# A causal attention layer's step order: exponentials and maxima taken before the step's long matmul unit, key copies issued by SP, normalized rows stored in two parts

## The reference

```python
x = x + layernorm(attention(layernorm(x)))      # 16 query heads of 32, one key/value head, causal
x = x + layernorm(moe(layernorm(x)))            # 8 experts, top 2, and a shared expert
# attention: q = xn @ q_w.T + q_b ; k, v likewise (32 wide)
#   scores = q k^T / sqrt(32), later keys masked ; softmax ; times v ; @ o_w.T + o_b
```

## Time and profile before

| | us |
|---|---|
| median of 3 runs | 2262.08 |
| profiled execution, its own time | 2262.99 |
| its span, first to last instruction | 2261.2 |
| attention, from the page's slices and the timeline | 0 to about 892 |
| routing, experts, shared expert | about 892 to 2261 |
| TensorE busy in the whole span | 2015.1 (89%) |
| VectorE, ScalarE, GpSimd busy | 1043.0, 713.6, 468.7 |
| mean granted TensorE clock | 0.946 of full |

### The profile page before, as it was taken

One profiled execution on the slowest core, in us unless ns is written; L12 is line 12 of the kernel. 1 busy time (PEld: TensorE's weight loads), 2 busy tenths in 40 slices (PEclk: granted clock), 3 DMA queues, 4 the chain that ended last, 5 costly groups with the idle time before them and its releaser, 6 DMA issues. The chain is left out here.

```text
span 2261.2 us, 30875 instructions
## 1 busy us (share of the span) xinstructions
PE 2015.1 (89%) x10858; PEld 1534.2 (68%) x10858; DVE 1043.0 (46%) x2158; ACT 713.6 (32%) x1350; POOL 468.7 (21%) x1044
## 2 busy tenths in 40 slices
PE   4988989888888982399999999999999999999995
PEld 3655555565555541377788788878888888888884
DVE  3555655565555533744454555534424333233243
ACT  2434444444444341143433344422111111111111
POOL 1223232332423232111101111000121120220212
PEclk9799999999999986599998999999999999999998
DMA  5133351615243221434443555443120230221202
GB/s 172 51 98 114 99 164 67 193 53 159 84 129 112 84 94 74 152 102 171 162 174 138 190 171 186 145 168 97 46 103 19 94 112 19 94 73 48 103 19 93
DMA packets 107018, 250.36 MB, mean 111 GB/s; under 512 B 10752, under 2 KB 25344, under 8 KB 99616
## 3 DMA queue, kind: packets, MB, share of 16 engines
q1 hardware_dynamic: 92064, 207.73, 26.9%
q0 software_dynamic: 11520, 37.76, 5.3%
q10 hardware_dynamic: 3328, 3.41, 0.7%
HBM read 165.76 MB, written 79.69 MB: 109 GB/s over the span
## 5 line engine op out<-in xcount | busy, mean ns | idle before, releaser
L1223 PE MATMUL ex_bank<-ex_xT,ex_gu 128*128 128x512 f32 (+14 forms) x1656 | 345.5, 367 | 5.0 <-DVE ex_xT L1257 5.0
L1223 PEld LDWEIGHTS ex_bank<-ex_xT,ex_gu 128*128 128x128 f32 (+1 forms) x1656 | 277.1, 183 | 69.3 <-DVE ex_xT L1257 5.4
L632 DVE TENSOR_REDUCE at_nmax<-at_bank 128x1 f32<-128x384 f32 (+3 forms) x512 | 229.7, 479 | 123.3 <-PE at_bank L407 122.9
L1273 DVE TENSOR_TENSOR sh_silu<-sh_silu,sh_bank 128x512 f32<-128x512 f32 x88 | 60.6, 688 | 457.6 <-ACT sh_silu L1266 451.0
L1223 PE MATMUL sh_bank<-sh_xT,sh_gate 128*128 128x512 f32 x1056 | 255.4, 391 | 6.8 <-DVE sh_dn L1679 5.2
L1235 PE MATMUL sh_bank<-sh_dn,sh_act 128*128 128x512 f32 x1056 | 254.3, 390 | 0.0
L1223 PE MATMUL sh_bank<-sh_xT,sh_up 128*128 128x512 f32 x1056 | 253.6, 389 | 0.0
L827 ACT ACTIVATE at_PT<-at_bank 128x512 f32<-128x512 f32 (+1 forms) x384 | 194.7, 515 | 175.8 <-PE at_bank L420 164.4
L1266 ACT ACTIVATE sh_silu<-sh_bank 128x512 f32<-128x512 f32 x88 | 52.7, 599 | 592.4 <-PE sh_bank L1223 547.0
L1223 PEld LDWEIGHTS sh_bank<-sh_xT,sh_gate 128*128 128x128 f32 x1056 | 199.0, 189 | 49.4 <-issue 8.1
L1235 PEld LDWEIGHTS sh_bank<-sh_dn,sh_act 128*128 128x128 f32 x1056 | 197.6, 188 | 43.7 <-DVE sh_act L1282 2.9
(11 more groups left out here) (227 smaller groups left out, 2581.6 us busy)
## 6 DMA issues: line engine op xcount, KB each, us to landing
ex_gu_in<-gu_in SPq DMA_DIRECT2D x23, 1408.0 KB, 9.2
at_Qs<-q_dram SPq DMA_DIRECT2D x96, 256.0 KB, 4.7
ys<-sh_yk SPq DMA_DIRECT2D x17, 1024.0 KB
q_dram<-at_q_h SPq DMA_DIRECT2D x64, 256.0 KB, 3.6
xnT<-at_xT SPq DMA_DIRECT2D x16, 1024.0 KB, 5.7
sh_xT<-xnT SPq DMA_DIRECT2D x16, 1024.0 KB
ex_dn_in<-dn_in SPq DMA_DIRECT2D x23, 512.0 KB, 9.6
at_x_in<-x_in SPq DMA_DIRECT2D x8, 1024.0 KB, 5.3
```

The source lines that it names most:

```text
L632: last = nc.vector.tensor_reduce(nmax[:, s % 2, i:i + 1], S_ps[u][:, col:col + (i + 1) * P], AX_X, ALU.max, negate=True)
L1223: last = self.nc.tensor.matmul(self.gate_up_ps[c % 2][which][0:m, 0:w], cols(i, k), self.xT[j][:, k, 0:w], start=(step == 0), stop=(step = ...
L1273: nc.vector.tensor_tensor(silu[c % 2][0:m, 0:w], silu[c % 2][0:m, 0:w], gate_up_ps[c % 2][1][0:m, 0:w], ALU.mult).then_inc(s["product"], 1)
```

## The change

1. In the 12 steps that are not in `PAIRED` (steps 1, 2, 9 and 10, whose units come in two halves) VectorE takes the maxima of unit 2, and ScalarE the exponentials of unit 2, ahead of `first_low` and `first_high`.
2. `move_k` goes from ScalarE's program to SP's. For sequence 0 its six transfers come before the first `spill_q`. KsT of sequence b comes between `spill_q(b, 3)` and `move_q(b, 3)`; KsS of sequence b+1 between `move_q(b+1, 1)` and `spill_q(b+1, 2)`, behind a wait for the last query scores of sequence b.
3. In SP's list x_res is loaded after the stores of xnT and xn2; `move_q(b+1, 0)` comes before the store of x1; the store of xn2 of sequence b-2 stands in turn b behind that of xnT (before: of sequence b-1 in turn b, near the end).
4. ScalarE normalizes tiles 0 and 1 of x1 of sequence b-1 at the end of step 15 of turn b, and tiles 2 and 3 at the end of step 0 of turn b+1.

```diff
--- before.py
+++ after.py
@@ -269,6 +269,8 @@
 
         Q_STEP = {12: 0, 13: 1, 15: 2, 0: 3}
 
+        PAIRED = (1, 2, 9, 10)
+
         def head(b, s, lag):
             return (b, s - lag) if s >= lag else (b - 1, s - lag + H)
 
@@ -308,6 +310,11 @@
                 for half in range(2):
                     sp.dma_start(q_dram[half, c], q_h[c % 2][half][:].bitcast(F32)).then_inc(q_spilled[c], 16)
 
+            def move_k(n, Ks, moved):
+                for at, half in ((0, 0), (1, 0), (2, 1)):
+                    sp.dma_start(Ks[HD * at:HD * at + HD, :].bitcast(F32),
+                                  vk_h[half][HD:2 * HD, :].bitcast(F32)).then_inc(moved, 16)
+
             def move_q(n, c):
                 if has(n - 1):
                     sp.wait_ge(shifted, 3 * (H * (n - 1) + HG * (c + 1)))
@@ -318,6 +325,9 @@
 
             sp.wait_ge(xT1_ps, C)
             sp.dma_start(x_in[:], seq(x, 1)).then_inc(x_in_s, 16)
+            sp.wait_ge(qkv_lo, 1)
+            move_k(0, KsS, kS_moved)
+            move_k(0, KsT, kT_moved)
             spill_q(0, 0)
             spill_q(0, 1)
             move_q(0, 0)
@@ -327,35 +337,37 @@
             sp.wait_ge(w_split, 6)
 
             def turn(b):
-                if has(b - 1):
-                    if has(b - 2):
-                        sp.wait_ge(x1_ready, QT * (b - 1))
-                    sp.dma_start(x_res[:], seq(x, b - 1)).then_inc(x_res_s, 16)
                 if has(b):
                     spill_q(b, 3)
+                    if has(b - 1):
+                        sp.wait_ge(shifted, 3 * H * b)
+                        move_k(b, KsT, kT_moved)
                     move_q(b, 3)
                 if has(b - 2):
                     sp.wait_ge(xT2_lo, C * (b - 1))
                     for half in range(2):
                         sp.dma_start(xnT_out[bass.ds(b - 2, 1), half].rearrange("o p c t -> p (o c) t"),
                                      xT[half][:].bitcast(F32)).then_inc(xnT_stored, 16)
+                    sp.dma_start(seq(xn_out, b - 2), xn2[:]).then_inc(xn2_moved, 16)
+                if has(b - 1):
+                    if has(b - 2):
+                        sp.wait_ge(x1_ready, QT * (b - 1))
+                    sp.dma_start(x_res[:], seq(x, b - 1)).then_inc(x_res_s, 16)
                 if has(b + 2):
                     sp.wait_ge(xT1_ps, C * (b + 2))
                     sp.dma_start(x_in[:], seq(x, b + 2)).then_inc(x_in_s, 16)
                 if has(b + 1):
                     spill_q(b + 1, 0)
+                    move_q(b + 1, 0)
                 if has(b - 1):
                     sp.wait_ge(x1_ready, QT * b)
                     sp.dma_start(seq(x1_out, b - 1), y[:]).then_inc(x1_stored, 16)
                 if has(b + 1):
-                    move_q(b + 1, 0)
                     spill_q(b + 1, 1)
                     move_q(b + 1, 1)
+                    sp.wait_ge(scores, 3 * H * (b + 1))
+                    move_k(b + 1, KsS, kS_moved)
                     spill_q(b + 1, 2)
-                if has(b - 1):
-                    sp.wait_ge(xn_ready, QT * b)
-                    sp.dma_start(seq(xn_out, b - 1), xn2[:]).then_inc(xn2_moved, 16)
-                if has(b + 1):
                     move_q(b + 1, 2)
 
             turns(sp, turn)
@@ -751,10 +763,15 @@
                     maximum(b, s, 1)
                     norm_steps(b, s, 1)
                     spread_inverses(b, s)
-                    first_low(b, s)
-                    maximum(b, s, 2)
-                    norm_steps(b, s, 2)
-                    second_low(b, s)
+                    if s in PAIRED:
+                        first_low(b, s)
+                        maximum(b, s, 2)
+                        norm_steps(b, s, 2)
+                        second_low(b, s)
+                    else:
+                        maximum(b, s, 2)
+                        norm_steps(b, s, 2)
+                        first_low(b, s)
                     take_sums(b, s)
                     scale_mixed(b, s)
                     take_v(b, s)
@@ -790,12 +807,6 @@
                 staged, halves, _ = WEIGHTS[part]
                 act.wait_ge(w_in[part], 16)
                 nc.scalar.activation(halves[0][:], staged, ACT.Copy).then_inc(w_hi, 1)
-
-            def move_k(n, Ks, moved):
-                act.wait_ge(qkv_lo, 5 * n + 1)
-                for at, half in ((0, 0), (1, 0), (2, 1)):
-                    act.dma_start(Ks[HD * at:HD * at + HD, :].bitcast(F32),
-                                  vk_h[half][HD:2 * HD, :].bitcast(F32)).then_inc(moved, 16)
 
             high_weights(0)
             high_weights(1)
@@ -809,8 +820,6 @@
             scale_vk(0, bank[0])
             high_q(0, 0, bank[1])
             high_q(0, 1, bank[2])
-            move_k(0, KsS, kS_moved)
-            move_k(0, KsT, kT_moved)
             high_q(0, 2, bank[3])
 
             def exponentials(b, s, tb):
@@ -880,19 +889,17 @@
             def turn(b):
                 for s in range(H):
                     exponentials(b, s, 0)
-                    if s == 2 and has(b) and has(b - 1):
-                        act.wait_ge(shifted, 3 * H * b)
-                        move_k(b, KsT, kT_moved)
                     take_row(b, s)
                     high_mixed(b, s)
                     exponentials(b, s, 1)
                     move_row(b, s)
-                    first_high(b, s)
-                    exponentials(b, s, 2)
-                    second_high(b, s)
-                    if s == H - 1 and has(b + 1):
-                        act.wait_ge(scores, 3 * H * (b + 1))
-                        move_k(b + 1, KsS, kS_moved)
+                    if s in PAIRED:
+                        first_high(b, s)
+                        exponentials(b, s, 2)
+                        second_high(b, s)
+                    else:
+                        exponentials(b, s, 2)
+                        first_high(b, s)
                     if s in (7, 8) and has(b + 1):
                         for i in range(2 * s - 14, 2 * s - 12):
                             normalize(x_in, x_in, 0, b + 1, i, x_normed)
@@ -901,8 +908,11 @@
                             normalize(y, y, 1, b - 1, i, y_normed)
                     if s == H - 1 and has(b - 1):
                         act.wait_ge(xn2_moved, 16 * b)
-                        for i in range(QT):
+                        for i in range(2):
                             normalize(xn2, y, 2, b - 1, i, xn_ready)
+                    if s == 0 and has(b - 2):
+                        for i in range(2, QT):
+                            normalize(xn2, y, 2, b - 2, i, xn_ready)
 
             turns(act, turn)
 
```

## The result

| | before | after |
|---|---|---|
| median, us | 2263.73 (2256.04 to 2266.34, 4 runs) | 2193.14 (2189.26 to 2199.07, 4 runs) |
| profiled execution, its own time | 2262.99 | 2199.07 |
| its span | 2261.2 | 2197.3 |
| turns 1 to 7 | 690.3 | 633.2 |
| TensorE busy; mean granted clock | 2015.1; 0.946 | 1988.5; 0.948 |

The ratio is 0.9696 (95% interval 0.9661 to 0.9731): 3.0% faster, 70.6 us by the medians and 63.9 us by the two profiled executions. The forecast was 2188, 5 us lower. That is closer than its terms deserve: several were wrong by 10 to 25 us, in both directions.

A forecast was written before the change was run, and what follows sets the result against it. TensorE was taken as the pacer of attention, so only its idle or slow time could be gained; the terms summed to -74.6 us, taking 2263.0 to 2188 us, with a range of 2167 to 2214.

The forecast's parts named there:

- What bounds the kernel: Attention, turns 1 to 7: TensorE is the pacer, busy 599 of 690 us; later stages counted unchanged.
- Maxima ahead: VectorE in unpaired steps: TensorE's waits for maxima go, 35.6 us of 38.1; bounds 0 and 38.1.
- exponentials ahead: ScalarE in unpaired steps: key scores' waits for exponentials go, 17.2 us of 20.5; bounds 0 and 20.5.
- The high half moved behind costs nothing: ScalarE, unpaired steps: free, since its unit ends 2 to 3 us later than the exponential of 0.36 us.
- KsS by SP: Start of each turn: earlier key issue leaves about 1.0 us wait per turn, 9.6 of 16.6 us go.
- Rival 1: Keys stay as late as now, behind the queries in SP's queue; total 2205 us; chance 0.18.
- KsT and step 2: Steps 2 and 3: waits for KsT, the row and part of xT go, 7 us; bounds 0 and 10.7.
- The clock: project_q in steps 0 and 12: two thirds of 17.3 us of clock dips go, 11.5; bounds 5 and 17.3.
- First turn: Turn 0: SP issues the keys; 1.5 us off the 7.3 us wait for the first queries.
- Normalizing in two parts: Steps 0 and 1: two moved ACTIVATEs cost 0.85 us in turns 2 to 7, +5.1; bounds 0 and 9.2.
- Rows stored later: Last turn: xn's store behind both xnT parts delays the next stage by 2.7 us; bounds 2 and 4.3.
- Rivals 3 and 4: Rival 3 (0.10): VectorE takes the maximum's place in steps 5 to 8, 2202 us; rival 4 (0.05): SP queue bounds, slower.

The follow-up runs named there:

- the orders alone: Kernel before with only the VectorE and ScalarE orders changed (maxima and exponentials of unit 2 ahead of the long unit): 2206.11 us, ratio 0.9767.
- Keys first: Kernel after, with KsS ahead of move_q(b+1, 1) in SP's list instead of behind it: 2167.50 us, ratio 0.9598.
- two tiles ahead: Keys first, plus tiles 2 and 3 normalized ahead of high_q in step 0 and xn2 stored ahead of its transposes: 2161.94 us, ratio 0.9559.

## Why the prediction came out as it did

- *What bounds the kernel*: right. The stage behind attention hardly moved, and all of the gain lies in what TensorE spent idle or slow.
- *Maxima ahead, -35.6; exponentials ahead, -17.2*: the mechanism was right (steps 5 to 8 last 4.40 us, against 4.6 foretold, and L390's waits fell from 55 to 7), the sizes were not. The sum was made from recorded waits, and each stall costs about 0.2 us more than its record: steps 5 to 8 alone gave 20.3 us for 28 waits that sum to 14.4. Against that stood a cost that the prediction did not have: 9.8 us of waits stay at L402, where it left 1.1. 3.3 of them are the copies of keys and values under GpSimd's additions. Split between the two, the terms were far off: about 62 and 4 us, not 36 and 17, since each was priced as if the other wait had no part in it. "The high half moved behind costs nothing" was wrong twice: what comes after the earlier exponential falls on VectorE's copies, and the two tiles that are normalized behind the high half end too late for step 1.
- *KsS by SP, -9.6*: against the kernel before the wait grew by 6.2. Two things are in that: the orders alone, with shorter steps, made it 25.0, and SP's issue took off 6.1 (28.9 to 22.8, or 2.2 from the 25.0). The forecast left 1.0 us in each turn, and 3.3 stayed. The step that failed is "SP's queue still holds the queries of move_q(b+1, 1), 0.75 MB, issued at 413.1": that time was taken over from the trace of before, but the list was edited ahead of it. The second spill left 10.6 us ahead of turn 4 instead of 12.1 and stood behind 1.75 MB, its landing took 6.8 instead of 4.6 us, and the queries that wait for it left 3.7 us later in the turn, right ahead of the keys. The three issues took 1.8 us, not 1.3. Rival 1 had the place behind the queries, not the later issue, and was given 0.18; its total of 2205 was too high because the other terms were too small.
- *KsT and step 2, -7*: right. Its wait and that for the row are gone, step 2 lost 7.9 us, step 3 gained 0.3 with the wait for mixed_f.
- *The clock, -11.5*: step 12's share came (3.0 us in every turn, 5.4 saved, 1.1 of it in turn 0), step 0's did not (11.9 over became 10.3 over), since the wait ahead of it grew. Together 7.0. Keys first shows that it was there to be had.
- *First turn, -1.5*: the first query scores begin at 41.5 instead of 44.5 us and their wait is 6.1 instead of 7.3. With the shorter steps of turn 0, turn 1 begins 11.8 us earlier; the terms for this stretch (3.8 and 1.7 of the two orders' and 1.5) make 7.0.
- *Normalizing in two parts, +5.1*: right in sign, a little small: step 1 is 7.5 us longer in all, with the wait for xn in its row (4.2 us in 6); undoing the part took 6.2 of them back.
- *Rows stored later, +2.7*: right. GpSimd opens the next stage 2.77 us behind the last logits (823.73 to 826.50), before 0.54: 2.2 us.
- *Rivals 3 and 4*: VectorE took no place in steps 5 to 8 (no wait there), and the keys came about 3 us too late (5.2 at most), far from the 11.7 from which the change would cost time.

Against the profiled execution the sum was 10.7 us too low. The keys (15.8), the clock (4.5) and the normalizing (2.4) were put too well by 23 us; with the other terms at their measured sizes the two orders are left with about 57 us in turns 1 to 7 for 47 forecast there, 10 too few; what lies outside those turns gave 7.1 us (1.1 of it clock) for 4.3. The profiled execution is the slowest of its four, and the median forgave another 6. That the centre was near is in large part luck: terms that were 10 and more too large met terms that were as much too small.

## What to carry to other kernels

Where a queue's list is edited, work out the issue time of everything in it anew, and count the bytes that stand ahead of a small urgent transfer, those that hold up its predecessors' landings too: a late one at the turn's start takes back what is gained ahead of it (the exponentials' order gave nothing measurable with the keys late, and 4 us of turns without). Count a removed stall of TensorE a little above its record (0.2 us each here), and the clock behind a long one separately. Where two waits stand in one step, price them together: the second can take up what the first gives back. When an engine's work moves earlier, ask what it releases on a third engine, and on whose ports that falls.

## What was not expected of the hardware

- A stall of TensorE recorded as 0.47 us costs 0.70 us of the step; 28 of them, recorded as 14.4 us, cost 20.3.
- A cast of 64x512 fp32 within SBUF went from 0.42 to 1.26 us, and a subtraction with two SBUF inputs from 0.68 to 1.66, beside GpSimd's additions; reduces from PSUM did not change.
- A wait of 1.8 us ahead of the query scores of step 13 stood in four turns of most kernels. In the kernel after the unit behind it ran its 3.0 us each time, with keys first and two tiles ahead it took 3.7 to 4.3 in three, at a granted clock of 0.81 over the step in turn 2. Steps 3 to 5 of turn 0 took 8.2 us in two kernels (keys first, and with two tiles ahead) and 11.4 to 12.5 in the others; the granted clock was 1.00 in keys first and 0.63 in the kernel after, with waits of 3.5 and 3.0 us. What decides these stays open.
